# The last merge's output projection: weights held and 512 tokens streamed, a ScalarE copy, and TensorE transposes, in place of tokens held and 96 channels streamed

## What is computed

```python
y = y * jax.nn.silu(z)
return jnp.einsum('bld,cd->blc', y, W_out)
...
x = x + _L3_conv_ref(_gn(x), ...)
```

## Time and profile before

| | us |
|---|---|
| median of 3 runs | 35931.14 |
| lowest, highest | 35928.1, 35933.79 |
| the profiled execution's own time | 35929.24 |
| its span, first to last instruction | 35927.5 |

### The profile page before, as it was taken

One profiled execution on the slowest core, in us unless ns is written; L12 is line 12 of the kernel. 1 busy time (PEld: TensorE's weight loads), 2 busy tenths in 40 slices (PEclk: granted clock), 3 DMA queues, 4 the chain that ended last, 5 costly groups with the idle time before them and its releaser, 6 DMA issues. The chain is left out here.

```text
span 35927.5 us, 322721 instructions
## 1 busy us (share of the span) xinstructions
PE 25878.4 (72%) x73032; PEld 8083.4 (22%) x73032; DVE 32944.5 (92%) x14881; ACT 19018.1 (53%) x23286; POOL 30835.7 (86%) x7804
## 2 busy tenths in 40 slices
PE   5777777777766777777777766777777777766777
PEld 2222222222222222222222222222222222222224
DVE  5999999999977999999999977999999999976993
ACT  4555555555534555555555534555555555534551
POOL 1999999999961999999999951999999999964994
PEclk7888888888888888888888888888888888887886
DMA  4666666666675666666666675666666666675665
GB/s 154 176 175 175 177 176 178 176 176 176 176 223 168 177 176 175 177 176 179 176 177 178 176 219 167 177 177 175 176 177 176 178 176 176 177 222 181 176 176 149
DMA packets 2423696, 6402.41 MB, mean 178 GB/s; under 512 B 703824, under 2 KB 875728, under 8 KB 2411728
## 3 DMA queue, kind: packets, MB, share of 16 engines
q1 hardware_dynamic: 2421968, 6387.69, 67.0%
HBM read 2986.75 MB, written 764.47 MB: 104 GB/s over the span
## 5 line engine op out<-in xcount | busy, mean ns | idle before, releaser
L1283 POOL TENSOR_TENSOR h<-h,c 128x2048 f32<-128x2048 f32 x4992 | 20774.7, 4182 | 242.8 <-DVE h L1083 150.5
L1083 DVE TENSOR_TENSOR_SCAN h<-decay,state,slots 128x1024 f32<-128x1024 f32 x6240 | 14306.8, 2335 | 120.4 <-ACT state L1227 9.3
L988 PE MATMUL psy<-h,t_fold 128*32 128x512 f32 x40000 | 10449.2, 672 | 6.1 <-POOL h L1283 5.9
L1122 ACT ACTIVATE decay<-delta,na 128x1024 f32<-128x1024 f32 x6248 | 7115.4, 1146 | 3014.3 <-DVE h L1083 2775.0
L1079 DVE TENSOR_TENSOR_SCAN h<-slots,state,made 128x1024 f32<-128x1024 f32 x3744 | 8551.7, 2327 | 108.3 <-ACT slots L1122 106.1
L1304 POOL TENSOR_TENSOR made<-du,b 128x2048 f32<-128x2048 f32 x1872 | 7823.4, 4179 | 669.4 <-DMA b<-bcdram 669.4
L911 PE MATMUL slots<-bc,pick 96*128 96x512 bf16 x6248 | 2327.4, 461 | 7905.6 <-DVE h L1079 6853.2
L1056 DVE TENSOR_TENSOR slots<-du,slots 128x2048 f32<-128x2048 f32 x3120 | 7165.4, 2297 | 706.9 <-PE slots L911 298.6
L1122 ACT ACTIVATE slots<-delta,na 128x1024 f32<-128x1024 f32 x3744 | 4166.0, 1114 | 5010.9 <-DVE h L1083 5009.4
L988 PEld LDWEIGHTS psy<-h,t_fold 128*32 128x32 f32 x40000 | 2202.4, 120 | 7785.7 <-issue 7522.8
L1296 POOL TENSOR_TENSOR du<-delta,u 128x1024 f32<-128x1024 f32 x628 | 1478.0, 2353 | 2356.3 <-ACT delta L1176 2356.3
(11 more groups left out here) (111 smaller groups left out, 20168.8 us busy)
## 6 DMA issues: line engine op xcount, KB each, us to landing
delta<-delta SPq DMA_DIRECT2D x10048, 128.0 KB, 2.6
du<-du SPq DMA_DIRECT2D x10048, 128.0 KB, 3.0
b<-bcdram SPq DMA_DIRECT2D x7520, 128.0 KB, 2.8
c<-bcdram SPq DMA_DIRECT2D x6720, 128.0 KB, 2.9
u<-useq SPq DMA_DIRECT2D x212, 1536.0 KB, 6.9
yseq<-ybuf SPq DMA_DIRECT2D x624, 512.0 KB, 2.7
ya<-yseq SPq DMA_DIRECT2D x420, 512.0 KB, 4.9
yb<-yseq SPq DMA_DIRECT2D x360, 512.0 KB, 5.9
```

The lines of the kernel that those rows point to most:

```text
L988: mm = pe.matmul(psy[rows, cols], T["fold"][:, :], h[v % H_RING][:, c, cols], start=(v % QUADS == 0), stop=(v % QUADS == QUADS - 1), skip_ ...
L1083: dve.tensor_tensor_scan(out, decay[s % DECAY_RING][:, order], slot[s % 2][:, order], first, ALU.mult, ALU.add).then_inc(sem["h_ready"], 1)
L1122: act.activation(dst, delta4[j % DELTA_RING][:, s % 2, :], ACT.Exp, scale=na[q][:, k:k + 1])\
L1283: pool.tensor_tensor(both[:, :, 0:CH], both[:, :, 1:], c4[g][:, order].unsqueeze(1).broadcast_to((P, 2, CH)), ALU.mult)\
```

## The change

In the last merge alone, `project` holds `wo` and streams 512 tokens into 96 channels x 512 tokens, for both images: two matmuls of 128 rows, two of 64 rows, and two that hold the 96 x 96 identity and stream `xr`. It writes to `outp` or, every other block, to two banks of `scale`. ScalarE copies that tile (96 x 1024) to the new `oc` (`take_block`). TensorE's new `turn` transposes the 8 pieces of 96 x 128 into 128 tokens x 96 channels in `cent`, and ScalarE copies these to `ob` (`put_tokens`), as L1597 did. `turn(c - 1)` is issued after `project(c)`, and `put_tokens(c - 1)` after `take_block(c)`. `project` waits for `taken` (of the block two before) in place of `x_done`; `x_done` comes from `put_tokens`. At a pair's end the order on TensorE is `project(7)`, `turn(6)`, raise `x_free`, `turn(7)`.

```diff
--- before.py
+++ after.py
@@ -1329,7 +1329,7 @@
     assert not (last and norm)
     names = ("w_in job_in0 job_in1 job_in2 job_in3 paired total_step x_in x_free gate_in0 gate_in1 "
              "centred_full squared copied var_full rooted inverted spread normed affine gated "
-             "out_full out_stored x_done x_stored")
+             "out_full out_stored x_done x_stored taken turned")
     NB = BANKS_L
     DEPTH = 4
 
@@ -1373,10 +1373,13 @@
         root = sb("root", [96, BANK])
         tn = [sb(f"tn{j}", [P, TILES, BANK]) for j in range(2)]
         ob = sb("ob", [P, 2, 4, DM]) if last else None
+        oc = [sb(f"oc{j}", [DM, 2, BANK]) for j in range(2)] if last else None
         cent = ctx.enter_context(nc.psum_tensor("cent" + W["tag"], [P, TILES, BANK], F32))
 
         scale = ctx.enter_context(nc.psum_tensor("scale" + W["tag"], [P, TILES, BANK], F32))
         outp = ctx.enter_context(nc.psum_tensor("outp" + W["tag"], [P, 2, BANK], F32))
+
+        outs = [outp, scale[:, 0:2, :]]
         y_v = yseq.rearrange("(k p c) t q l -> k p c t q l", p=PAIRS, c=NCH)
 
 
@@ -1494,7 +1497,10 @@
                 def project(p, c):
                     pe.wait_ge(sem["gated"], p * NB + (c + 3))
 
-                    pe.wait_ge(sem["x_done"], p * NB + (c + 1))
+                    if last:
+                        pe.wait_ge(sem["taken"], p * NB + (c + 1))
+                    else:
+                        pe.wait_ge(sem["x_done"], p * NB + (c + 1))
                     if last and c == 0:
                         pe.wait_ge(sem["x_in"], p * 16 + 16)
                     g = tn[c % 2]
@@ -1509,19 +1515,31 @@
                                            start=False, stop=True)
                     else:
                         for b in range(2):
+                            pe.matmul(outs[c % 2][0:DM, b, :], wo[:, 2 * b * DM:(2 * b + 1) * DM], g[:, 2 * b, :],
+                                      start=True, stop=False)
+                        for b in range(2):
                             rows = slice(64 * b, 64 * b + 64)
-                            for j in range(4):
-                                o = outp[:, b, j * DM:(j + 1) * DM]
-                                tok = slice(j * P, (j + 1) * P)
-                                pe.matmul(o, g[:, 2 * b, tok], wo[:, 2 * b * DM:(2 * b + 1) * DM],
-                                          start=True, stop=False)
-                                pe.matmul(o, g[rows, 1, tok], wo[rows, DM:2 * DM], start=False, stop=False)
-                                mm = pe.matmul(o, xr[:, b, c * BANK + j * P:c * BANK + (j + 1) * P],
-                                               T["ident"][0:DM, 0:DM], start=False, stop=True)
+                            pe.matmul(outs[c % 2][0:DM, b, :], wo[rows, DM:2 * DM], g[rows, 1, :],
+                                      start=False, stop=False)
+                        for b in range(2):
+                            mm = pe.matmul(outs[c % 2][0:DM, b, :], T["ident"][0:DM, 0:DM],
+                                           xr[:, b, c * BANK:(c + 1) * BANK], start=False, stop=True)
                     mm.then_inc(sem["out_full"], 1)
 
+                def turn(p, c):
+
+                    pe.wait_ge(sem["taken"], p * NB + (c + 3))
+
+                    pe.wait_ge(sem["x_done"], p * NB + (c + 1))
+                    for b in range(2):
+                        for j in range(4):
+                            mm = pe.transpose(cent[:, b, j * DM:(j + 1) * DM], oc[c % 2][:, b, j * P:(j + 1) * P],
+                                              T["ident"][0:DM, 0:DM])
+                    mm.then_inc(sem["turned"], 1)
+
 
                 pe.sem_inc(sem["out_full"], 2)
+                pe.sem_inc(sem["turned"], 2)
                 pe.sem_inc(sem["var_full"], 1)
                 pe.sem_inc(sem["spread"], 1)
                 pe.wait_ge(sem["w_in"], 96)
@@ -1540,11 +1558,14 @@
                                     project(p, c - 1)
                             else:
                                 project(p, c)
+                                if last and c:
+                                    turn(p, c - 1)
                         if norm:
                             project(p, NB - 1)
                         if last:
                             pe.wait_ge(sem["out_full"], p * NB + (NB + 2))
                             pe.sem_inc(sem["x_free"], 1)
+                            turn(p, NB - 1)
 
             @block.scalar
             def _(act):
@@ -1572,7 +1593,19 @@
                         act.activation(tn[c % 2][:, t, :], tn[c % 2][:, t, :], ACT.Identity, bias=lnb[:, t:t + 1],
                                        scale=lng[:, t:t + 1]).then_inc(sem["affine"], 1)
 
+                def take_block(p, c):
+                    act.wait_ge(sem["out_full"], p * NB + (c + 3))
+                    act.wait_ge(sem["turned"], p * NB + (c + 1))
+                    act.copy(oc[c % 2][:], outs[c % 2][0:DM, :, :]).then_inc(sem["taken"], 1)
+
+                def put_tokens(p, c):
+                    act.wait_ge(sem["turned"], p * NB + (c + 3))
+                    act.wait_ge(sem["out_stored"], p * (32 * NB) + 32 * (c + 1))
+                    act.copy(ob[:].rearrange("q b j d -> q b (j d)"), cent[:, 0:2, 0:4 * DM])\
+                        .then_inc(sem["x_done"], 1)
+
                 act.sem_inc(sem["copied"], 1)
+                act.sem_inc(sem["taken"], 2)
                 act.wait_ge(sem["w_in"], 96)
                 if not norm and not last:
                     return
@@ -1591,11 +1624,11 @@
                                 if c + 1 < NB:
                                     take(p, c + 1)
                             if last:
-                                act.wait_ge(sem["out_full"], p * NB + (c + 3))
-
-                                act.wait_ge(sem["out_stored"], p * (32 * NB) + 32 * (c + 1))
-                                act.copy(ob[:].rearrange("q b j d -> q b (j d)"), outp[:, :, 0:4 * DM])\
-                                    .then_inc(sem["x_done"], 1)
+                                take_block(p, c)
+                                if c:
+                                    put_tokens(p, c - 1)
+                        if last:
+                            put_tokens(p, NB - 1)
 
             @block.vector
             def _(dve):
```

## The result

The changed kernel takes 35771.17 us, the median of five runs (35759.99 to 35776.31), where the kernel before took 35933.79 beside it. The ratio is 0.9952, with a 95% interval of 0.9941 to 0.9963: it is about half a per cent faster. The medians are 163 us apart, and the interval reaches from 133 to 212. The forecast was 200 us, 35731, in a range of 35698 to 35830. Its direction and its range held; 37 us of the forecast gain didn't come.

The account below looks back on a forecast made before the run. TensorE was taken to bound the last merge within a pair, xr's load between pairs. Per pair 53.2 us saved less 3.1 lost, times 4, gave 200 us: 35929.2 becomes 35729, plus 1.9 is 35731; range 35698 to 35830.

Parts of the forecast that it names:

- The bound before: Last merge: TensorE bounds within a pair, 122.7 us; xr's load bounds between pairs, 19.86 of 23.4 us.
- the end of TensorE as the bound: Last merge: projection plus transposes take 7.2 us, half a block, so TensorE no longer bounds.
- The new wait: SP's queue: gate of block c+2 stands behind store_tokens(c-1), whose x_done now comes after project(c), turn(c-1) and second copy.
- P: A block's projection on TensorE: 6.1 us, between 4.8 at 2.4 GHz and 9.3 at 1.2 GHz.
- cold start of 6.55: Projection begun at the low clock: 3.63 us for its first four records, then 1.04 and 1.88 at full clock.
- the body: A pair from its first projection to the end of its last: 69.5 us, where it was 122.7.
- t: A block's eight transposes on TensorE: 1.1 us, upper bound 4.7.
- the rival drawn from it: Transposes don't count for the clock: every projection cold at 6.55 us, transposes 1.94; 171 us saved, 35760; chance 9%.
- D: Round from turn(c-1)'s end to project(c+2), through copy, x_done, gate and POOL: 11.9 or 14.0 us, two rounds interleaved.
- The end of a pair: xr's load waits for block 7's x_done, now behind two turns and two copies: 3.1 us lost per pair.
- The sum: Whole kernel: (53.2 - 3.1) x 4 = 200 us saved, giving 35731 us.
- The slower rival: Rounds don't interleave, a block takes 20.1 us: 109 us lost, 36040; chance 3%.

Follow-up runs that it names:

- e1_gate_first: Changed kernel with each store issued one block later on SP's queue: 35678.46 us, ratio to the kernel before 0.9928.
- e4_turn_at_once: Changed kernel with each block's transposes right behind its own projection and its put_tokens right behind its take_block: 35690.22 us, ratio to the kernel before 0.9931.
- e5_two_ob: Changed kernel with two output tiles ob, each with its own store semaphore, and unused tiles yb left out: last merge's stage 378.2 us, changed kernel 382.5.
- e6_two_names: Kernel before, plus the change's two more semaphores, made and cleared in every merge but used by none: 35935.94 us beside 35931.89, ratio 1.0001.
- e10_filler_two: Changed kernel with 4 filler matmuls into an unused bank behind the turn in blocks 2 and 4: last merge's stage 377.8 us.
- e3_filler: Changed kernel with 7 filler matmuls into an unused bank behind the turn in blocks 2, 4 and 6: last merge's stage 376.5 us.
- e7_filler_short: Changed kernel with 5 filler matmuls into an unused bank behind the turn in blocks 2, 4 and 6: last merge's stage 370.0 us.

## Why the prediction was right, and what it missed

- **The bound before, and the end of TensorE as the bound**: right. The new wait stands where it was put, in SP's order, and e1_gate_first and e4_turn_at_once removed it in two ways, each taking 78 to 81 us from the stage (of e4_turn_at_once's 78, 11 came from the ends of pairs).
- **P**: the parts were right, timeline of TensorE, one cold and one full projection:

```profile
35515.80 3.73 PE L1518 MATMUL scale<-tn,wo 128*96 128x512 f32 x4 [7.73 <-POOL tn L1726]
35519.46 2.02 PE L1522 MATMUL scale<-tn,wo 64*96 64x512 f32 x4
35521.41 2.04 PE L1525 MATMUL scale<-xr,t_ident 96*96 96x512 f32 x4
35523.28 0.82 PE L1536 MATMUL cent<-t_ident,oc 96*128 96x96 f32 x8
35523.94 1.88 PE L1518 MATMUL outp<-tn,wo 128*96 128x512 f32 x4
```

  L1525 costs what L1503 did; L1522 is 1.95 us from start to start when cold, 1.03 at full clock, and the prediction's cold start of 6.55 had it always at full clock: where it isn't, as here, a cold projection takes up to 7.6. Besides, the mean of 6.1 was applied to all blocks, and they aren't alike. The even ones take mostly 4.8 and so come early, and the idleness that the prediction spread over blocks 3 to 7 (4.7, 2.1, 2.6, 4.2 and 0.5 us) gathers ahead of the odd ones: 5.7 to 7.7 us ahead of blocks 3, 5 and 7, at most 1.1 ahead of 4 and 6. Those odd ones start cold, take 6.4 to 7.6 us, and are the ones in the chain. That is the mis-sized term of the body: the five projections in its chain (blocks 0, 1, 3, 5 and 7) take 32.6 us on average for the 30.5 forecast, and the body 70.9 to 73.5, 71.8 on average, for 69.5.
- **t**: 0.66 us from the start of the eight transposes to the next matmul, where 1.1 was taken. It isn't in the chain at all: the second copy waits for the take in front of it on ScalarE (1.0 us each), not for the transposes. The prediction had that copy as hidden, at nothing.
- **The page's rule**, that transposes don't engage the full clock (the Trainium skill, "TensorE: Matmul & The Clock Gate", Part 4): the rival drawn from it had t at 1.94 us and every projection cold. The trace disagrees with that: the granted clock through eight transposes, and the projection right behind them (1.88 us for its first four records), stand at full speed, and t is 0.66. Whether transposes alone would keep the clock up, a stretch of 0.6 us behind dense work can't tell; that they raised it is seen in the earlier trace rows alone. The stretch of those eight:

```profile
35502.00:35502.60 0.60, 0.60 (x9) 0.60 (x8) 0.00 (x0) 0.38 (x1) 0.00 (x0) 1.00 0.00 0
```

- **D**: right in sum, in part by luck. From the projection's end at 35722.47 to the next at 35735.45 are 13.0 us; t + 11.9 was 13.0. Ten of the twelve such rounds of odd blocks take 12.7 to 13.2 us, two take 13.7 and 14.3. But where the sum had t, 1.1 us, the chain has the take and its handover, 0.9: two errors of nearly the same size cancel.
- **The end of a pair**: 28.1 us from the last projection to the next first, forecast 23.4 + 3.1 = 26.5. The step that failed named two copies and two turns and put at nothing that the second copy writes the same `ob`, whose store has only just been issued: 2.35 us of waiting, in the chain above. e5_two_ob took 1.8 of it.
- **The sum**: some 2.3 us too little for a body and 1.6 for an end, 16 us in all: 184 us measured in the stage for 200 forecast. The other 21 of the missing 37 stand ahead of the stage. The prediction put nothing there ("The first pair's start is unchanged"), and kernels of the new form do start it 10 to 25 us later by the estimate under e6_two_names; why stays open. So the time landed in the range with one term of the change missing altogether.
- **The slower rival**, rounds that follow each other, didn't come: they interleave, as the starts of blocks show (in the second pair 8.1, 12.4, 8.1 and 12.4 us apart from block 3 on, where rounds in a row would be 20).

## What to carry to other kernels

Where an in-order queue waits for "the result is stored" before it prefetches the next input, software-pipelining the output by one block moves that wait behind the next block's work, and the input is late by it. Skew the queue with it: issue loads that need only a free buffer ahead of stores that need a result. And when a bound goes, cost the blocks behind the new gaps one by one, since here they were the ones that started at the low clock and the very ones in the chain.

## What the runs showed of the hardware

- Two matmuls of 64 rows on different rows of the array run together with weights held and 512 columns streamed: their records start in twos, 6 and 7 ns apart (from 35499.12 in the changed kernel), and all four take 1.03 us, where two of 96 rows, which share rows, take 1.80 (35500.15 to 35501.94).
- Eight fp32 transposes of 96 x 128 take 0.66 us at full clock. The nearest row suggested more (four of 128 x 96 in 0.65), but its duration holds the tail of the last one, as 0.82 does here; at full clock those start 0.11 to 0.15 us apart, these 0.08.
- A gap of 3.2 us behind dense work was enough for a cold start in e10_filler_two (block 5 of the first pair), one of 2.3 us was not in e3_filler, and one of 2.0 us was in e7_filler_short (3.40 us for the first four records of block 6 in the last pair), while behind 3.37 us in e1_gate_first block 4 of the last pair started at full clock (1.96 us): the length of the gap alone doesn't tell.
